# A routed expert layer: 28 tiles of 256 rows and 15 blocks of 128 rows in place of 39 tiles

## The chip, the core and the metric

The kernel runs on one core of one Trainium2 chip. The time is that of the device, in microseconds, for one launch. The kernel before took 417.74 us (median of 3 runs, 417.27 to 418.27).

## What is computed

`x` has 16 sequences of 256 tokens with 128 features, 4096 tokens in all. Everything is float32. One block of a transformer is computed: a modulated layer norm, a causal linear attention with 16 heads, a gated residual, and then the same around a layer of eight routed experts:

```python
h = rmsnorm(x @ W_in.T, in_norm_w)                 # 4096 x 128
logits = h @ Wr.T                                  # 4096 x 8
_, idx = top_k(logits + expert_bias, 2)            # two experts for each token
gates = softmax of the two chosen logits, else 0
for e in range(8):
    gate = silu(h @ Wg[e].T)                       # 128 -> 512
    up = h @ Wu[e].T                               # 128 -> 512
    oe = rmsnorm(gate * up @ Wd[e].T, enorm_w[e])  # 512 -> 128
    out = out + gates[:, e:e + 1] * oe
x = x + gb * (rmsnorm(out, out_norm_w) @ W_out.T)
```

The kernel computes an expert only for the tokens that chose it: 8192 rows (4096 tokens, two experts each). How many rows go to which expert is known only while the kernel runs.

## The kernel before

Three stages follow each other. **Attention and routing** goes through the 16 sequences in a software pipeline. It writes each normed row of a token, as a high and a low float16 half, into the DRAM buffer `dispatched` (`hbuf`), once for each of its two experts; every expert has a region of its own there. GpSimd does this with 64 indirect transfers of 128 rows (L547). **The expert stage** reads the rows back in tiles, computes gate, up and down, and writes the results to `expert_rows` (`ybuf`) in the order of the tokens. **The last stage** reads them in four transfers (L465), mixes the two results of a token, norms them and projects them.

**Tiles and tables.** A tile is `R = 256` rows of one expert. In the worst case the 8192 rows need `TILES = (8192 + 8*255) // 256 = 39` tiles, and always 39 are computed: unused ones read filler rows, whose results go to rows of `ybuf` that nobody reads. After the last sequence VectorE takes the counts of the experts (`total`, L1255), works out where each region ends (`tail`, L1257) and makes the table of tiles (L1260 to L1279: `tile_row`, the first row of each tile, and `tile_expert`). SyncE (L413) and ScalarE (L777) fill up the end of each region with 256 filler rows, 129 KB, in four transfers each. SyncE waits for all scatters, all filler and the table (L417 to L420), loads the table's rows into registers (L444 in the chain of waits) and starts on the tiles.

**The expert stage.** Its engines run the same order, written by hand, in turns of four tiles: a first turn, a loop `Fori(1, TURNS - 1)` and a last turn of three tiles. For a tile `t`:
- SyncE brings the 256 rows into SBUF turned by two DMA transposes, one for the high and one for the low half (L430), into slot `t % 4`, once tile `t - 4` no longer needs it. It also loads where the results go (`to_place`, L437).
- TensorE does `gate_up` (L1702) in halves of 256 of the 512 hidden columns: gate half 0, up half 0, gate half 1, up half 1. Each product of 128 hidden columns is three matmuls of 256 columns (high weights by high rows L1712, high by low L1713, low by high L1714): 24 of them in a tile. Then `down` (L1717) of tile `t - 1`: 24 matmuls of 128 columns (L1727 to L1729). Which weights are read depends on a register with the expert's number, so the addresses are worked out on the queue of TensorE as the kernel runs: the trace has register operations (ALU_OP, FUSED_REGOPS) under these lines.
- ScalarE does silu of a half (`gate`, L788), the high float16 half of the product (`high_part`, L794) and the sums of squares of the results of tile `t - 2` (`square`, L800).
- VectorE does the product of gate and up (`gated`, L1312), its low float16 half (`low_part`, L1319) and the scaling of the results (`weigh`, L1326).
- GpSimd scatters the results: two indirect transfers of 128 rows for each tile (L570).

G, U and Y are two PSUM banks each. TensorE may write a half of G or U when ScalarE and VectorE have read what stood in it two halves before.

## Time and profile before

| | us |
|---|---|
| median of 3 runs (lowest to highest) | 417.74 (417.27 to 418.27) |
| the profiled execution | 417.46 |
| its span, first to last instruction | 415.5 |
| from the start to the first matmul of the expert stage | 213.34 |
| from there to the start of its last matmul | 160.56 |
| after that | 41.6 |

The span is shown by the profile from its first to its last instruction; the execution took 1.96 us more. Busy time of an engine is that of its instructions. A matmul's duration is its way through the array, and several are under way at once: what a matmul costs in a dense row is the distance of the starts.

### The profile page before, as it was taken

The numbers are of one execution on the slowest core, as the hardware profiler recorded it, in microseconds if no ns is written. First come the engines' busy times: TensorE is split into PE (matmuls) and PEld (weight loads), VectorE is DVE, ScalarE is ACT, GpSimd is POOL, SyncE is SP. The second block draws the span as 40 slices with busy tenths as digits, with TensorE's granted clock in tenths as the row PEclk, the third lists the DMA queues.
The fourth block names the chain that finished last, engine by engine and source line by source line (L and its number), as shares of the span: only waits on it lengthen the run. The fifth ranks groups of instructions, "written<-read, shape, count | busy, mean of one in ns | idle before, by whom it ended". The sixth has DMA issues, their size and how long they took to land.

```text
span 415.5 us, 12907 instructions
## 1 busy us (share of the span) xinstructions
PE 353.6 (85%) x3750; PEld 308.6 (74%) x3751; DVE 321.0 (77%) x1029; ACT 292.0 (70%) x814; POOL 245.1 (59%) x221
## 2 busy tenths in 40 slices
PE   3799999999999999984049999999999999990464
PEld 2588887888888888873039989889899999980343
DVE  4078898899999999885828878787787778780686
ACT  4344769888888888744617778778778787873595
POOL 1957566788888888865541554554545455463341
PEclk9999999999999999995559999999999999997698
DMA  7997000000000000011412323233232232213833
GB/s 237 399 361 293 4 6 21 27 29 27 25 25 25 25 25 25 28 52 36 144 38 48 66 66 69 65 69 70 57 70 64 64 71 56 65 34 101 350 98 95
DMA packets 46563, 35.68 MB, mean 86 GB/s; under 512 B 36291, under 2 KB 42070, under 8 KB 45750
## 3 DMA queue, kind: packets, MB, share of 16 engines
q1 hardware_dynamic: 41718, 21.21, 18.4%
q0 software_dynamic: 4544, 9.39, 7.0%
q10 hardware_dynamic: 272, 4.72, 3.0%
q8 instruction: 15, 0.25, 0.3%
q14 instruction: 14, 0.11, 0.1%
HBM read 18.69 MB, written 13.47 MB: 77 GB/s over the span
## 4 chain that ended last, share of the span: by engine, by line
PE 52%; DVE 20%; issue 9%; DMA 8%; ACT 7%; POOL 2%; DVEq 1%; SPq 0%; ACTq 0%; POOLq 0%
PE bank L1712 9%; PE bank L1713 8%; PE bank L1714 8%; PE bank L1465 5%; DVE prod L953 4%; PE bank L1727 4%; PE bank L1729 4%; PE bank L1728 4%; DMA gates_bc<-gate_rows 4%; ACT junk L846 2%; PE bank L1543 2%; DVE st L877 1%; DVE rows L1014 1%; DVE wmaxs L1049 1%; DMA dispatched<-rows,pos 1%
## 5 line engine op out<-in xcount | busy, mean ns | idle before, releaser
L570 POOL DMA_INDIRECT expert_rows<-late,to_place x78 | 81.8, 1049 | 82.9 <-DVE late L1326 70.3
L1712 PE MATMUL bank<-late,w_hi 128*128 128x256 f16 x312 | 86.3, 277 | 14.8 <-DMA late<-dispatched 13.4
L1714 PE MATMUL bank<-late,w_lo 128*128 128x256 f16 x312 | 86.2, 276 | 0.0
L1713 PE MATMUL bank<-late,w_hi 128*128 128x256 f16 x312 | 86.2, 276 | 0.0
L1312 DVE SCALAR_TENSOR_TENSOR kv<-bank,uscale,kv 128x512 f32<-128x512 f32 x78 | 58.5, 750 | 32.1 <-ACT kv L788 18.6
L547 POOL DMA_INDIRECT dispatched<-rows,pos x64 | 67.3, 1051 | 26.7 <-issue 18.4
L529 POOL TENSOR_TENSOR kv<-kv,v 128x1024 f32<-128x1024 f32 x32 | 67.6, 2134 | 16.2 <-ACT kv L691 16.2
L1465 PE MATMUL bank<-cst,kv 128*128 128x128 f32 x576 | 74.6, 281 | 1.1 <-POOL kv L529 0.9
L1465 PEld LDWEIGHTS bank<-cst,kv 128*128 128x128 f32 x576 | 69.4, 195 | 1.8 <-POOL kv L529 1.0
L788 ACT ACTIVATE kv<-bank,descale 128x512 f32<-128x512 f32 x78 | 53.6, 687 | 23.3 <-PE bank L1714 19.3
L794 ACT ACTIVATE kv<-kv 128x512 f16<-128x512 f32 x78 | 48.8, 625 | 16.9 <-DVE kv L1312 11.4
L1319 DVE TENSOR_TENSOR kv<-kv 128x512 f16<-128x512 f32 x78 | 54.1, 693 | 5.6 <-ACT kv L794 3.6
L1727 PE MATMUL bank<-late,kv 128*128 x312 | 54.3, 219 | 0.5 <-DVE kv L1319 0.5
L1728 PE MATMUL bank<-late,kv 128*128 x312 | 54.3, 219 | 0.0
L1729 PE MATMUL bank<-late,kv 128*128 x312 | 54.3, 219 | 0.0
L953 DVE TENSOR_TENSOR prod<-bank,qT 128x384 f32<-128x384 f32 x96 | 49.6, 544 | 0.0
L1712 PEld LDWEIGHTS bank<-late,w_hi 128*128 x312 | 30.9, 99 | 20.1 <-issue 16.4
L1714 PEld LDWEIGHTS bank<-late,w_lo 128*128 x312 | 31.0, 99 | 3.9
L1713 PEld LDWEIGHTS bank<-late,w_hi 128*128 x312 | 31.0, 99 | 3.5
L612 ACT ACTIVATE xn<-x_all,nmr,rs 128x128 f32<-128x128 f32 (+1 forms) x64 | 27.8, 482 | 5.8 <-DVE nmr L894 5.5
L1727 PEld LDWEIGHTS bank<-late,kv 128*128 128x128 f16 x312 | 30.5, 98 | 1.1 <-issue 0.6
L1728 PEld LDWEIGHTS bank<-late,kv 128*128 128x128 f16 x312 | 30.5, 98 | 0.4
(231 smaller groups left out, 737.4 us busy)
## 6 DMA issues: line engine op xcount, KB each, us to landing
late<-wguT ACTq DMA_DIRECT2D x1, 4096.0 KB, 16.0
late<-expert_rows SPq DMA_DIRECT2D x1, 2064.0 KB, 11.0
gates_bc<-gate_rows SPq DMA_DIRECT2D x1, 2048.0 KB, 15.7
wd<-wdT SPq DMA_DIRECT2D x1, 2048.0 KB, 24.4
out<-kv SPq DMA_DIRECT2D x16, 128.0 KB, 1.8
late<-dispatched SPq DMA_TRANSPOSE x78
expert_rows<-late,to_place POOLq DMA_INDIRECT x78
late<-expert_rows SPq DMA_DIRECT2D x1, 1032.0 KB, 6.6
```

Source lines behind the costliest of these rows:

```text
L529: nc.gpsimd.tensor_tensor(kvt[:, 0:HD, :, :], k_in, v_in.to_broadcast([P, HD, H, HD]), ALU.mult).then_inc(kv_done[t], 1)
L547: pool.indirect_dma_start(hbuf, bass.IndirectOffsetOnAxis(ap=pos[:, p, t * K + k:t * K + k + 1], axis=0), rows[:, p, t, k, :], None).then_ ...
L570: pool.indirect_dma_start(ybuf, bass.IndirectOffsetOnAxis(ap=to_place[:, s, r:r + 1], axis=0), yt[:, s, r, :], None).then_inc(y_scat[s], 16)
L953: nc.vector.tensor_tensor(prod[:, t, cc * THIRD * P:(cc + 1) * THIRD * P].rearrange("p (e i) -> p e i", i=P), cum, qT[:, p, t * P:(t + 1) ...
L1312: nc.vector.scalar_tensor_tensor(gu[:, h, :], U[h], uscale[:], sg[:, h, :], ALU.mult, ALU.mult).then_inc(gu_done, 1)
L1465: last = mm(CUM[cc][:, j * P:(j + 1) * P], kv[:, p, t, e * D:(e + 1) * D], tri, start=True, stop=True)
L1712: mm(o, w_hi[:, w], hi, start=True, stop=False)
L1713: mm(o, w_hi[:, w], lo, start=False, stop=False)
L1714: last = mm(o, w_lo[:, w], hi, start=False, stop=True)
L1727: mm(o, gu_hi[:, s % 2, h, g], wd_hi[:, w], start=(f == 0 and r == 0), stop=False)
L1728: mm(o, gu_lo[:, s % 2, h, g], wd_hi[:, w], start=False, stop=False)
L1729: last = mm(o, gu_hi[:, s % 2, h, g], wd_lo[:, w], start=False, stop=(f == FC - 1 and r == RB - 1))
```

## The change

The expert stage computes 28 tiles of 256 rows (7 turns of four, the last turn being a turn like the others) and then 15 blocks of 128 rows. `TILES = (64 - 8) // 2 = 28`; `BLOCKS = (8192 + 8*127) // 128 - 56 = 15`. The regions' ends are filled with 128 rows. A tile now holds 256 rows only where the expert has more than 128 left for it. The 15 blocks have a table of their own, made by VectorE in 19 instructions behind the low halves of the down weights (L1284) and ahead of its first tile. The blocks are written out, not in a loop. On every engine their order is that of the tiles, one block in place of one half of a tile: TensorE does gate (12 matmuls of 128 columns), up (12) and then down of the block two before (12). The rows of a tile or block come by one DMA transpose for both halves. The weights' addresses are worked out in bytes. The diff below goes by engine: the constants; SyncE's filler (ScalarE's four transfers change alike), its tiles and its blocks; GpSimd, ScalarE, VectorE and TensorE.

```diff
-TILES = (TOK * K + E * (R - 1)) // R
-TURNS = -(-TILES // TURN)
-SPARE = TILES - TOK * K // R
+TILES = (TOK * K // P - E) // RB
+TURNS = TILES // TURN
+BLOCKS = (TOK * K + E * (P - 1)) // P - RB * TILES
+SPARE = (TOK * K + E * (P - 1)) // P - TOK * K // P
...
-    c[:, C_J:C_J + TOK // R] = np.arange(TOK // R) * R
+    c[:, C_J:C_J + TOK // R] = np.arange(TOK // R) * R + P
+    c[:, C_J0:C_J0 + TOK // R] = np.arange(TOK // R) * R
...
-                sp.dma_start(hbuf[bass.ds(row, R), :].rearrange("(p j) w -> p (j w)", p=16),
-                             filler[e * R:(e + 1) * R, :].rearrange("(p j) w -> p (j w)", p=16)).then_inc(filled, 16)
+                sp.dma_start(hbuf[bass.ds(row, P), :].rearrange("(p j) w -> p (j w)", p=16),
+                             filler[e * P:(e + 1) * P, :].rearrange("(p j) w -> p (j w)", p=16)).then_inc(filled, 16)
...
-                for half in range(2):
-                    sp.dma_start(hT3[:, s, half], hbuf16[bass.ds(row, R), half * D:(half + 1) * D],
-                                 transpose=True).then_inc(slot_ld[s], 16)
+                sp.dma_start(hT3[:, s], hbuf16[bass.ds(row, R), 0:2 * D], transpose=True).then_inc(slot_ld[s], 16)
...
+            def load_block(j, reg):
+                s = j % TURN
+                row = sp.snap(reg, min_val=0, max_val=HROWS - P)
+                sp.wait_ge(u3_ps, 2 * (TILES - TURN + j) + 2 if j < TURN else 2 * TILES + j - TURN + 1)
+                sp.dma_start(hT3[:, s, :, 0:P], hbuf16[bass.ds(row, P), 0:2 * D],
+                             transpose=True).then_inc(slot_ld[s], 16)
...
+            for j in range(BLOCKS):
+                s = j % TURN
+                pool.wait_ge(y_done[s], TURNS + j // TURN + 1)
+                pool.indirect_dma_start(
+                    ybuf, bass.IndirectOffsetOnAxis(ap=to_place[:, s, 0:1], axis=0),
+                    yt[:, s, 0, :], None).then_inc(y_scat[s], 16)
...
+            def block_gate(j):
+                act.wait_ge(g_ps, 2 * TILES + j + 1)
+                act.wait_ge(gu_done, 2 * TILES + j - 1)
+                nc.scalar.activation(sg[:, j % 2, :], G[j % 2], ACT.Silu, scale=descale[:]).then_inc(sg_done, 1)
+            def block_high(j):
+                act.wait_ge(gu_done, 2 * TILES + j + 1)
+                act.wait_ge(y_ps, TILES - 1 + j // 2 if j < TURN else TILES + j - TURN + 1)
+                nc.scalar.activation(gu_hi[:, j // 2 % 2, j % 2, :], gu[:, j % 2, :], ACT.Copy).then_inc(guhi_done, 1)
+            def block_square(j):
+                act.wait_ge(y_ps, TILES + j + 1)
+                act.wait_ge(ysq_done, RB * TILES + j)
+                nc.scalar.activation(junk3[:], Y[j % 2][:, 0:D], ACT.Square, scale=ydesc[:],
+                                     accum_out=yt[:, j % TURN, 0, D:YW]).then_inc(ysq_done, 1)
...
+            for j in range(2, BLOCKS):
+                block_high(j - 1)
+                if j == 2:
+                    for r in range(RB):
+                        square(TILES - 1, TURN - 1, TURNS - 1, r)
+                else:
+                    block_square(j - 3)
+                block_gate(j)
+            block_high(BLOCKS - 1)
+            for j in range(BLOCKS - 3, BLOCKS):
+                block_square(j)
...
+            for j in range(2, BLOCKS):
+                if j % TURN == 2:
+                    dve.load(block_ex[j // TURN % 2], block_expert[0:1, j - 2:j - 2 + TURN])
+                block_low(j - 1)
+                block_gated(j)
+                if j == 2:
+                    weigh(TILES - 1, TURN - 1, TURNS - 1, dve.snap(last_ex[1], min_val=0, max_val=E - 1))
+                else:
+                    block_weigh(j - 3, expert_of_block(j - 3))
...
+            def columns_of(w, e, per_expert, at):
+                return w.bitcast(U8)[:, bass.ds(e * (2 * per_expert) + 2 * at, 2 * P)].bitcast(F16)
...
-                    w = bass.ds(e * F + (part * E * F + (h * (FC // 2) + c) * P), P)
-                    mm(o, w_hi[:, w], hi, start=True, stop=False)
-                    mm(o, w_hi[:, w], lo, start=False, stop=False)
-                    last = mm(o, w_lo[:, w], hi, start=False, stop=True)
+                    wh, wl = (columns_of(w[:], e, F, part * E * F + (h * (FC // 2) + c) * P) for w in (w_hi, w_lo))
+                    mm(o, wh, hi, start=True, stop=False)
+                    mm(o, wh, lo, start=False, stop=False)
+                    last = mm(o, wl, hi, start=False, stop=True)
...
+            def block_gate_up(j, e, part):
+                s = j % TURN
+                if part == 0:
+                    pe.wait_ge(slot_ld[s], 16 * (TURNS + j // TURN + 1))
+                hi, lo = hT3[:, s, 0, 0:P], hT3[:, s, 1, 0:P]
+                pe.wait_ge((sg_done, gu_done)[part], 2 * TILES + j - 1)
+                for c in range(FC):
+                    o = (G, U)[part][j % 2][:, c * P:(c + 1) * P]
+                    wh, wl = (columns_of(w[:], e, F, part * E * F + c * P) for w in (w_hi, w_lo))
+                    mm(o, wh, hi, start=True, stop=False)
+                    mm(o, wh, lo, start=False, stop=False)
+                    last = mm(o, wl, hi, start=False, stop=True)
+                last.then_inc((g_ps, u3_ps)[part], 1)
+            def block_down(j, e):
+                pe.wait_ge(y_done[(j + 2) % TURN], TURNS + (j + 2) // TURN)
+                pe.wait_ge(gulo_done, 2 * TILES + j + 1)
+                o = Y[j % 2][:, 0:D]
+                for f in range(FC):
+                    g = slice(f * P, (f + 1) * P)
+                    hi, lo = gu_hi[:, j // 2 % 2, j % 2, g], gu_lo[:, j // 2 % 2, j % 2, g]
+                    wh, wl = (columns_of(w, e, FC * D, f * D) for w in (wd_hi, wd_lo))
+                    mm(o, hi, wh, start=(f == 0), stop=False)
+                    mm(o, lo, wh, start=False, stop=False)
+                    last = mm(o, hi, wl, start=False, stop=(f == FC - 1))
+                last.then_inc(y_ps, 1)
...
+            for j in range(BLOCKS):
+                if j % TURN == 0:
+                    pe.load(block_ex[j // TURN % 2], block_expert[0:1, j:j + TURN])
+                block_gate_up(j, expert_of_block(j), 0)
+                block_gate_up(j, expert_of_block(j), 1)
+                if j == 1:
+                    down(TILES - 1, TURN - 1, TURNS - 1, pe.snap(last_ex, min_val=0, max_val=E - 1))
+                elif j > 1:
+                    block_down(j - 2, expert_of_block(j - 2))
+            for j in range(BLOCKS - 2, BLOCKS):
+                block_down(j, expert_of_block(j))
```

## Rows read from the trace of the kernel before

**Rows 1.** The page: busy time by engine, with its share of the span and instructions.

```profile
PE 353.6 (85%) x3750; PEld 308.6 (74%) x3751; DVE 321.0 (77%) x1029; ACT 292.0 (70%) x814; POOL 245.1 (59%) x221
```

**Rows 2.** Stretches: busy us (and instructions) of each engine, granted clock, DMA.

```profile
193.00:213.00 20.00, 2.61 (x16) 1.66 (x13) 13.75 (x47) 8.07 (x14) 10.38 (x9) 0.50 0.29 90
230.60:327.80 97.20, 96.07 (x1152) 88.43 (x1152) 77.33 (x122) 77.66 (x193) 51.26 (x49) 1.00 0.31 66
327.80:374.20 46.40, 45.61 (x552) 41.92 (x552) 36.54 (x58) 36.64 (x94) 24.76 (x24) 1.00 0.25 56
...
392.60:413.00 20.40, 13.05 (x82) 9.83 (x82) 17.93 (x72) 17.16 (x79) 7.04 (x12) 1.00 0.32 92
```

**Rows 3.** Timeline of TensorE: start, us, engine, line, operation, what ended idle time.

```profile
214.16 0.42 PE L1713 MATMUL bank<-late,w_hi 128*128 128x256 f16 x1
...
285.80 0.27 PE L1714 MATMUL bank<-late,w_lo 128*128 128x256 f16 x1
285.91 0.22 PE L1727 MATMUL bank<-late,kv 128*128 x1
285.97 0.22 PE L1728 MATMUL bank<-late,kv 128*128 x1
...
327.86 0.28 PE L1712 MATMUL bank<-late,w_hi 128*128 128x256 f16 x1 [0.17 <-issue]
...
373.90 0.22 PE L1729 MATMUL bank<-late,kv 128*128 x1
```

**Rows 4.** Timelines of VectorE and ScalarE in one tile of the loop.

```profile
286.27 0.75 DVE L1312 SCALAR_TENSOR_TENSOR kv<-bank,uscale,kv 128x512 f32<-128x512 f32 x1
287.06 0.63 ACT L794 ACTIVATE kv<-kv 128x512 f16<-128x512 f32 x1 [0.40 <-DVE kv L1312]
287.61 0.37 ACT L800 ACTIVATE junk<-bank,ydesc 128x128 f32<-128x128 f32 x1
288.18 0.69 ACT L788 ACTIVATE kv<-bank,descale 128x512 f32<-128x512 f32 x1
288.97 0.75 DVE L1312 SCALAR_TENSOR_TENSOR kv<-bank,uscale,kv 128x512 f32<-128x512 f32 x1 [0.56 <-ACT kv L788]
```

**Rows 5.** TensorE's queue, 279.2 to 281.25: operation, count, duration ns, first and last start.

```profile
L1712 PEldq FUSED_REGOPS  x8: 46/46/46, 279.2 to 281.0; - x8
L1714 PEldq ALU_OP  x8: 32/32/36, 279.4 to 281.1; - x8
```

**Rows 6.** The same queue, table of experts, whole run.

```profile
L1698 PEldq TENSOR_LOAD <-tile_expert x10: 329/338/518, 205.4 to 359.2; - x10
```

**Rows 7.** The queue and the array at down's high weights (L1727), 281.2 to 282.5.

```profile
L1727 PEldq FUSED_REGOPS  x4: 46/46/46, 281.3 to 282.2; - x4
...
L1727 PE MATMUL bank<-late,kv x4: 219/219/219, 281.9 to 282.5; 128*128 x4
```

**Rows 8.** The chain of waits ahead of the expert stage: start, us, what.

```profile
204.20 4.89 DMA dispatched<-rows,pos
...
209.59 1.21 SPq L430
...
213.34 0.39 PE bank L1712
```

**Rows 9.** Issues that write `dispatched`, 199 to 209.4, and the page's median to landing.

```profile
L547 POOL DMA_INDIRECT dispatched<-rows,pos x5: 952/955/959, 198.3 to 204.2; - x5
L777 ACTq DMA_DIRECT2D dispatched<-filler x4: 530/619/657, 201.3 to 203.7; - x4
...
dispatched<-rows,pos POOLq DMA_INDIRECT x64, 2.3
```

**Rows 10.** Timeline of VectorE: the first tile's first product.

```profile
216.12 0.75 DVE L1312 SCALAR_TENSOR_TENSOR kv<-bank,uscale,kv 128x512 f32<-128x512 f32 x1 [6.00 <-PE bank L1714]
```

**Rows 11.** Timelines behind the last matmul: GpSimd, SyncE.

```profile
378.53 0.96 POOL L570 DMA_INDIRECT expert_rows<-late,to_place  x1 [0.30 <-issue]
...
381.16 1.77 SPq L465 DMA_DIRECT2D late<-expert_rows  x4
```

195 lines of the change are left out of this document (137 added, 58 removed).

## The prediction

> **What bounds the kernel now.** I read the busy times first. TensorE is busy 85% of the span, the most [rows 1], but that is an average over stages. By stretches, TensorE is busy 96.07 of 97.20 us inside the expert stage's loop at full clock [rows 2], with VectorE and ScalarE near 80%: this stage is bound by TensorE. Its timeline gives the price. A matmul of 256 columns starts 0.11 us after the one before, one of 128 columns 0.056 us after [rows 3]. A tile is 24 of each: 2.62 + 1.34 = 3.96 us. Over a turn of four come 0.2 to 0.3 us in which the queue loads the next experts (0.17 idle in the row at 327.86). The expert stage starts at 213.34, turn 7 (tile 28) at 327.86, and the last matmul ends at 373.90 + 0.22 = 374.12 [rows 3]. So the last 11 tiles, with one down carried over, cost 46.26 us.
>
> **Part 1: 11 tiles become 15 blocks.** By matmuls alone a block is 36 x 0.056 = 2.0 us, so 15 blocks with the carried down take 31.6 us and 14.7 us would be saved. I do not forecast that, because two things stand above 2.0 us.
>
> *The ring of ScalarE and VectorE.* In a block ScalarE does high(j-1), square(j-3), gate(j) and then at once high(j), which needs gated(j) of VectorE, which needs gate(j). No second half lies between, as in a tile. Start to start in the trace: gated to high 0.79, high to square 0.55, square to gate 0.57, gate to gated 0.79 [rows 4]. The ring is 2.70 us a block, and TensorE cannot go faster for long, as it has only two banks ahead.
>
> *TensorE's own queue.* Each product of three matmuls needs two register operations for its two weight addresses. In one tile's gate and up, 16 of them start within 1.9 us [rows 5], when nothing else held the queue: 0.24 us a product, 0.12 each, hardly depending on the matmuls between. In a tile this hides behind three matmuls of 256 columns, 0.33 us. In a block the three matmuls take 0.167 us, and the queue needs about 0.23. A block has 12 products, 24 operations. With 0.115 each (the rows hold waits too, so I go below 0.12): 2.76 us. Two places (start of gate, start of down) wait on two semaphores, so one wait stands as an instruction of its own; no row prices it, between nothing and one more 0.12; I take 0.10, near the register operations, 0.20 a block. Every fourth block the queue loads four experts, 0.34 us [rows 6], with the work on their numbers some 0.6 (estimated from the 0.2 to 0.3 us that a turn loses although the queue is ahead), so 0.15 a block. Sum 3.1; I take 3.05 us a block. Bytes in place of elements can turn the 46 ns operation into the 32 ns one [rows 5], 8 x 0.014 = 0.1 us a block, and two addresses a product remain. From below the ring bounds the block (2.70). From above, every operation is of the long kind and each of the three uses of a block's expert works out its own product: 24 x 0.13 + 0.2 + 0.15 = 3.5.
>
> So 15 x 3.05 = 45.75. Add the carried down (8 operations, 1.0). Subtract the lead that the queue has at that point: in the loop the first operation of down starts at 281.3 and its matmul at 281.9, the last at 282.2 for a matmul behind 282.5 [rows 7], 0.6 growing to some 0.8; I take 0.8. At the end down(14) waits for high and low of block 14, 0.35, and the last product drains, 0.25. Sum 46.55 against 46.26: **+0.3 us**. Seven row blocks fewer are computed, and the queue takes it back.
>
> VectorE and GpSimd keep up: one scatter of 0.96 + 0.30 us a block [rows 11] stands against 3.05.
>
> **Part 2: the first 28 tiles.** Their matmuls, waits and turns are the same; nothing on the path. SyncE's transposes are hidden there.
>
> **Part 3: half the filler.** The last scatter is issued at 204.20 and lands 4.89 us later [rows 8], where 2.3 is the median of 64 [rows 9]. What is new beside it are eight filler transfers of 129 KB, issued 201.3 to 203.7 [rows 9] (four by ScalarE, four alike by SyncE). With half the bytes the last scatter should land at its median, 206.5, the filler by 206.5 to 207.2. SyncE's wait ends up to 2.6 us earlier; I take **-2.2** (bounds -2.6 and 0).
>
> What is late next? The table of tiles is done at about 205, no. VectorE gets 19 small instructions (some 0.26 us each with their waits, 5 us) behind the low weights, in front of its first product. It has 6.00 us of idle there [rows 10]. With the start 2.6 us earlier it is late by 1 to 2 us, but TensorE needs that product only when up of tile 1 begins, 3 us after it is done now, so nothing. If that cover were gone: up to 1.5 us, once.
>
> **Part 4: one transpose.** The first tile waits for two issues, of 1.21 us and as much again, and landing [rows 8]. If one issue of 1.2 carries both halves, the first tile comes 1.2 us earlier; if its length goes with the rows of each half, nothing, and a little later if a half can no longer start alone (+0.3). I take **-0.4**.
>
> Here a rule of the Trainium skill can be weighed: "DMA: Bandwidth & Descriptors", Rules for kernel authors, says to coalesce many small transfers, since small ones mostly pay overhead. By it the whole second issue would go, and the sum would be 0.8 us lower. The rows only show that a transfer of 1.2 us issue is not followed at once by its data; they cannot decide it.
>
> **Part 5: the tail.** The last two scatters belong to the last tile, and GpSimd was a tile behind: the last begins at 378.53, 4.41 us after the last matmul [rows 3, 11]. After, the last block has one scatter. Its square takes 0.57 [rows 4], its weigh, half as wide as a tile's, some 0.35 (an estimate), and it finds GpSimd with at most one scatter in front: it begins 1.5 us after the last matmul. **-2.9** (bounds -3.2 and -1.5). From there on (378.53 to the load at 381.16 [rows 11] and the last stage) nothing changes.
>
> **Sum.** 0.3 - 2.2 - 0.4 - 2.9 = -5.2 us. The rows come from an execution of 417.46 us (span 415.5), 0.28 below the median: **412.3 us**.
>
> **Rivals.**
> - *The ring alone bounds a block* (queue cheaper than I read it, for instance one address operation a product). 15 x 2.70 + 0.8 = 41.3, -5.0; with the rest -5.5: 407.0 us. For: the ring's steps are rows. Against: nothing in [rows 5] shows a product with one operation. 0.22.
> - *The clock falls in the blocks*, the case on the other side. TensorE would have some 65% of its time filled, with short gaps at each product. At the lower level, 1.2 GHz, a matmul of 256 columns costs 0.21 us (the row at 214.16) [rows 3], one of 128 columns 0.107, and a block 36 x 0.107 = 3.85 us. 15 x 3.85 + 0.8 = 58.6, +12.3, minus 5.5: 424.3 us. It decides from about a third of the blocks at that clock, where 5.5 us are eaten. Against: from 392.6 to 413.0 TensorE is busy 13.05 of 20.40 us, 64%, at clock 1.00, while the clock of 0.50 goes with 2.61 of 20 us [rows 2]. 0.08. The Trainium skill speaks for it: "TensorE: Matmul & The Clock Gate", A second HAM failure mode: psum-queue depth-cycling, tells of a kernel whose brief idling between groups of matmuls made the clock swing between the two levels. The stretch at 392.6 does not bear that out here.
> - *The queue is dearer* (3.4 us a block: all operations of the long kind, products worked out anew, or the straight code of 15 blocks fetched too slowly). 51.8, +5.6, and the gain is gone: 417.5 us. For: the waits and the table are estimates, a tenth of the 3.05. Against: in the last turn, straight code too, TensorE stayed dense (the stretch from 327.80) [rows 2]. 0.14; beyond 3.5 us a block it would be slower.
> - *The front gives nothing* (the scatter's 4.89 us are not the filler's): 412.3 + 2.6 = 414.9 us. 0.06.
>
> The forecast keeps 0.50, with a range of its own from 410.3 to 415.0 (2.9 to 3.25 us a block).
>
> **Chances.** A measurement of this kernel can tell about 0.2%, 0.8 us. Faster: 0.50 + 0.22 + 0.06 and a fifth of the dear queue, 0.81. Same: 0.07, from the dear queue. Slower: 0.12, the clock and the dearest queue. The range that should hold 8 in 10 reaches from the ring with a full front, 406.3, to the dear queue, 417.5.
>
> **What would show it.** In the changed kernel the block stretch has a clock of 1.00 and matmuls in threes: 0.056, 0.056, then a gap, 0.23 us from first to first, with idle time put down to "issue" on TensorE or its weight loads; blocks start 3.05 us apart. If they stand 2.70 apart with the idle time behind ScalarE and VectorE, the ring was right. Blocks of 2.0 us would show both wrong. The first transpose should be issued near 207.4, the first matmul stand near 210.7, and the last scatter begin 1.5 us behind the last matmul. The forecast is wrong if the clock in the blocks shows 0.50, or if more than two register operations stand with a product.

## The result: 422.89 us in place of 417.5

The changed kernel took 422.89 us (median of 4 runs, 421.76 to 423.84), the kernel before, on the same chip, 417.5. The ratio is 1.010, with an interval of 1.006 to 1.015 (the two medians alone would give 1.013, inside it): slower by 1%, where I had forecast 412.3 us. The profiled execution took 423.49 us with a span of 421.7, 6.1 more than the span of before. The two traces, cut at the same points:

| stretch, us | before | after | difference |
|---|---|---|---|
| start to VectorE's copy of the counts (attention stage, unchanged) | 200.03 | 201.11 | +1.08 |
| to the first expert matmul | 13.31 | 11.00 | -2.31 |
| to the first matmul of tile 28, or of block 0 | 114.52 | 116.36 | +1.84 |
| to the end of the last expert matmul | 46.26 | 52.69 | +6.43 |
| to the first load of `expert_rows` | 7.04 | 4.31 | -2.73 |
| last stage | 34.36 | 36.19 | +1.83 |

### The profile page after: what moved, and what is told of

Read it like the earlier page. It is cut to its first block, busy times and chain, and to the rows that moved or that the text cites. A ratio compares the mean times of both kernels' runs of the same rounds, so it can differ in the third digit from the quotient of the medians.

```text
span 421.7 us, 12899 instructions
## 1 busy us (share of the span) xinstructions
PE 358.5 (85%) x3762; PEld 307.4 (73%) x3763; DVE 317.7 (75%) x1036; ACT 281.3 (67%) x786; POOL 237.3 (56%) x214
## 4 chain that ended last, share of the span: by engine, by line
PE 51%; DVE 24%; issue 9%; DMA 6%; ACT 6%; POOL 2%; DVEq 1%; ACTq 0%; POOLq 0%; SPq 0%
PE bank L1856 6%; PE bank L1858 6%; PE bank L1857 6%; PE bank L1605 4%; DVE prod L1023 4%; PE bank L1910 4%; DMA gates_bc<-gate_rows 4%; PE bank L1871 3%; PE bank L1872 3%; PE bank L1873 3%; PE bank L1912 2%; PE bank L1923 2%; PE bank L1911 2%; PE bank L1683 2%; DVE st L947 1%
## 5 line engine op out<-in xcount | busy, mean ns | idle before, releaser
L1856 PE MATMUL bank<-late,w_hi 128*128 128x256 f16 x224 | 62.5, 279 | 13.8 <-DMA late<-dispatched 11.0
L1858 PE MATMUL bank<-late,w_lo 128*128 128x256 f16 x224 | 62.4, 279 | 0.0
L1857 PE MATMUL bank<-late,w_hi 128*128 128x256 f16 x224 | 62.4, 279 | 0.0
L1412 DVE SCALAR_TENSOR_TENSOR kv<-bank,uscale,kv 128x512 f32<-128x512 f32 x56 | 41.8, 750 | 16.7 <-ACT kv L829 11.4
L829 ACT ACTIVATE kv<-bank,descale 128x512 f32<-128x512 f32 x56 | 38.3, 686 | 16.6 <-PE bank L1858 13.9
L835 ACT ACTIVATE kv<-kv 128x512 f16<-128x512 f32 x56 | 35.0, 626 | 14.8 <-DVE kv L1412 12.3
L1419 DVE TENSOR_TENSOR kv<-kv 128x512 f16<-128x512 f32 x56 | 38.8, 694 | 4.5 <-ACT kv L835 3.3
L1871 PE MATMUL bank<-late,kv 128*128 x224 | 39.0, 219 | 0.1
L1873 PE MATMUL bank<-late,kv 128*128 x224 | 39.0, 219 | 0.0
L1872 PE MATMUL bank<-late,kv 128*128 x224 | 39.0, 219 | 0.0
L1856 PEld LDWEIGHTS bank<-late,w_hi 128*128 x224 | 22.4, 100 | 17.9 <-issue 15.2
L1910 PE MATMUL bank<-late,w_hi 128*128 128x128 f16 x120 | 26.1, 219 | 2.9 <-issue 1.6
L1911 PE MATMUL bank<-late,w_hi 128*128 128x128 f16 x120 | 26.0, 218 | 0.0
L1912 PE MATMUL bank<-late,w_lo 128*128 128x128 f16 x120 | 25.9, 217 | 0.0
```

Of the source, the lines that this page charges most:

```text
L1856: mm(o, wh, hi, start=True, stop=False)
L1857: mm(o, wh, lo, start=False, stop=False)
L1858: last = mm(o, wl, hi, start=False, stop=True)
L1871: mm(o, gu_hi[:, s % 2, h, g], wh, start=(f == 0 and r == 0), stop=False)
L1872: mm(o, gu_lo[:, s % 2, h, g], wh, start=False, stop=False)
L1873: last = mm(o, gu_hi[:, s % 2, h, g], wl, start=False, stop=(f == FC - 1 and r == RB - 1))
```

## The profile after, against that of before

The page has hardly changed: TensorE at 85%, VectorE now at 75%.

```profile
PE 358.5 (85%) x3762; PEld 307.4 (73%) x3763; DVE 317.7 (75%) x1036; ACT 281.3 (67%) x786; POOL 237.3 (56%) x214
```

The stretches say where to look (busy us and instructions of PE, PEld, DVE, ACT, POOL; granted clock; DMA share and GB/s). They answer to [rows 2].

```profile
230.60:328.00 97.40, 96.38 (x1161) 88.83 (x1159) 77.61 (x123) 77.77 (x193) 51.13 (x48) 1.00 0.32 64
333.60:350.50 16.90, 15.49 (x187) 12.29 (x185) 8.85 (x15) 8.67 (x22) 7.19 (x7) 1.00 0.33 46
350.50:367.40 16.90, 15.24 (x178) 11.90 (x177) 8.16 (x16) 8.32 (x20) 4.79 (x5) 1.00 0.20 44
385.30:402.30 17.00, 8.14 (x35) 7.15 (x36) 8.87 (x34) 9.14 (x42) 4.96 (x8) 0.50 0.70 274
...
405.70:409.10 3.40, 3.19 (x15) 2.80 (x15) 2.73 (x12) 3.02 (x15) 1.58 (x3) 0.51 0.28 80
```

The tiles are as dense as before. In the blocks the clock is 1.00, so the clock does not bound a block. VectorE and ScalarE are idle half of the time; that alone would not rule their ring out, since two engines that wait for each other are both idle in turn. But no idle time of TensorE in the blocks is put down to them, only to "issue" (1.6 us from 333.6 to 374). TensorE looks 91% busy only because a matmul's 0.22 us on the array overlaps the next: 187 matmuls, at the 0.056 us of [rows 3], would need 10.5 of the 16.9 us. The last two lines are the last stage: its low clock lasts 17.0 us and comes back for 3.4, where before it was 13.6 us (379.0 to 392.6). Both kernels also end in a low stretch.

The timeline of TensorE (start, us, what, idle time and its cause) from block 0 to the last matmul; it answers to [rows 3].

```profile
328.47 0.22 PE L1910 MATMUL bank<-late,w_hi 128*128 128x128 f16 x1
...
341.02 0.23 PE L1910 MATMUL bank<-late,w_hi 128*128 128x128 f16 x1 [0.49 <-issue]
341.09 0.22 PE L1911 MATMUL bank<-late,w_hi 128*128 128x128 f16 x1
341.14 0.22 PE L1912 MATMUL bank<-late,w_lo 128*128 128x128 f16 x1
341.25 0.22 PE L1910 MATMUL bank<-late,w_hi 128*128 128x128 f16 x1
...
347.79 0.23 PE L1910 MATMUL bank<-late,w_hi 128*128 128x128 f16 x1
...
380.94 0.22 PE L1925 MATMUL bank<-late,kv 128*128 x1
```

Products start 0.23 us apart (341.02, 341.25), as predicted. Two blocks take 6.77 us (341.02 to 347.79), 3.39 each; those with a read of the table take 3.7 to 3.8. The average from block 4 on is 3.45 us.

What stood in TensorE's queue besides, all 15 blocks together (operation, count, ns least/median/most, first and last start); it answers to [rows 5, 6].

```profile
L1932 PEldq MOVE  x45: 29/29/38, 328.1 to 379.8; - x45
L1905 PEldq EVENT_SEMAPHORE  x15: 51/51/51, 328.2 to 375.3; - x15
L1917 PEldq EVENT_SEMAPHORE  x15: 51/51/51, 335.9 to 379.9; - x15
L1936 PEldq TENSOR_LOAD <-block_expert x4: 329/335/340, 327.7 to 368.0; - x4
L1910 PEldq FUSED_REGOPS  x30: 37/37/37, 328.3 to 376.4; - x30
L1912 PEldq ALU_OP  x120: 32/32/36, 328.4 to 377.2; - x120
```

A block has three MOVE (L1932 is the snap of the expert's number), two EVENT_SEMAPHORE (the waits of L1905 and L1917), 3 FUSED_REGOPS and 21 ALU_OP. The durations are not what they cost. From the start of one record of the queue to the start of the next, averaged over eight blocks (27.7 us): a weight load 0.037 us, an ALU_OP 0.061, FUSED_REGOPS 0.087, MOVE 0.088, EVENT_SEMAPHORE 0.114, TENSOR_LOAD 0.39. So 36 x 0.037 + 21 x 0.061 + 3 x 0.087 + 3 x 0.088 + 2 x 0.114 + 0.10 = 3.47 us a block. That this sum meets the time proves nothing: distances from start to start fill the time whatever the queue waits for. What speaks for the queue as the bound is that they hardly vary: each ALU_OP takes 60 or 61 ns, each MOVE 87 or 88, and 14 of the 16 EVENT_SEMAPHORE 106. Only the weight loads vary, from 13 to 208 ns; three in a block are followed by 57 ns or more, 0.18 us a block above the others (an estimate from these distances), and why stays open. Runs 5 to 9 test the rest.

Now the front. The timelines of VectorE, GpSimd and TensorE; they answer to [rows 10].

```profile
210.25 0.28 DVE L1360 TENSOR_TENSOR prod<-total,cst 1x128 f32<-1x128 f32 x1
210.57 0.27 DVE L1362 TENSOR_REDUCE nhalf<-prod 1x8 f32<-1x128 f32 x1
210.88 4.05 DVE L1363 TENSOR_SCALAR rest<-tstart 1x8 f32<-1x8 f32 x1
214.96 0.15 DVE L1364 SCALAR_TENSOR_TENSOR paired<-tend,rest 1x8 f32<-1x8 f32 x1
...
218.30 0.16 DVE L1384 SCALAR_TENSOR_TENSOR block_row<-cst,brow 1x16 int32<-1x16 f32 x1
219.28 1.41 DVE L1412 SCALAR_TENSOR_TENSOR kv<-bank,uscale,kv 128x512 f32<-128x512 f32 x2 [0.81 <-issue]
...
210.35 4.55 POOL L598 TENSOR_TENSOR gates_bc<-gates_bc,woutn 128x2048 f32<-128x2048 f32 x1 [4.07 <-DVE late L1353]
...
220.16 0.27 PE L1856 MATMUL bank<-late,w_hi 128*128 128x256 f16 x1 [1.74 <-DVE kv L1412]
```

One instruction on 8 numbers took 4.05 us. It ended at 214.93, when GpSimd's product of 128 x 2048 ended (214.90). That product stood there before too (210.27, 4.49 us), but VectorE was idle then. Now the table of the blocks is done at 218.46, the first product of gate and up starts at 219.28 in place of 216.12, and TensorE waits 1.74 us. This wait is what stands in the third row of the table of stretches (+1.84), where I had forecast nothing.

TensorE's first expert matmul (the first line, of its timeline) stands on its transfer, as before. But the chain of waits no longer goes through it: at this place it follows VectorE (the other lines). It answers to [rows 8].

```profile
212.11 0.39 PE L1856 MATMUL bank<-late,w_hi 128*128 128x256 f16 x1 [11.04 <-DMA late<-dispatched]
...
210.88 4.06 DVE rest L1363
219.28 0.76 DVE kv L1412
```

The transposes before tile 4, one in place of two, each as long to issue as one of two before:

```profile
L442 SPq DMA_TRANSPOSE late<-dispatched x4: 1186/1200/1312, 209.2 to 213.9; - x4
```

And the tail on the timelines of GpSimd and SyncE, which answers to [rows 11]: the last scatter starts 1.62 us after the end of the last matmul (381.16), where it was 4.41.

```profile
381.51 0.96 POOL L617 DMA_INDIRECT expert_rows<-late,to_place  x1 [0.30 <-issue]
382.78 0.96 POOL L617 DMA_INDIRECT expert_rows<-late,to_place  x1 [0.30 <-issue]
...
385.47 0.81 SPq L502 DMA_DIRECT2D late<-expert_rows  x2
```

## The experiments

They change the changed kernel, unless they say otherwise. Their ratios are to the kernel before on the same chip. "Front" is the time from the copy of the counts to the first matmul of tile 2, counting tiles from 0 (22.43 us before, 22.35 after), "block stage" that from the first matmul of tile 28 or block 0 to the end of the last (46.26 and 52.69).

| kernel | us | ratio, interval | front | blocks, mean from block 4 on |
|---|---|---|---|---|
| 1 another form | 422.93 | 1.010, 1.006 to 1.014 | 22.29 | 3.45 |
| 2 GpSimd later | 419.97 | 1.001, 0.999 to 1.004 | 20.30 | 3.45 |
| 3 filler of 256 | 424.08 | 1.011, 1.006 to 1.015 | 22.36 | 3.45 |
| 4 two transposes | 423.09 | 1.009, 1.006 to 1.012 | 22.35 | 3.59 |
| 5 light queue | 418.86 | 0.998, 0.994 to 1.002 | 24.00 | 3.04 |
| 6 snaps alone | 420.84 | 1.005, 1.003 to 1.008 | 22.36 | 3.18 |
| 7 waits alone | 420.80 | 1.006, 1.003 to 1.008 | 22.35 | 3.22 |
| 8 elements | 427.69 | 1.020, 1.015 to 1.025 | 24.03 | 3.64 |
| 9 fixed expert | 413.68 | 0.986, 0.982 to 0.991 | 22.35 | 2.96 |
| 10 fixed, scatter's wait moved | 415.67 | 0.992, 0.988 to 0.995 | 24.01 | 3.06 |
| 11 changed kernel again | 422.97 | 1.009, 1.006 to 1.013 | 24.02 | 3.45 |
| 12 kernel before again | 430.66 | 1.002, 0.998 to 1.006 | 22.36 | |
| 13 both repairs | 425.44 | 0.989, 0.985 to 0.992 | 20.29 | 3.16 |
| 14 and scatter's wait moved | 426.17 | 0.989, 0.986 to 0.992 | 20.29 | 3.11 |
| 15 and gate ahead of square | 426.14 | 0.990, 0.986 to 0.994 | 20.30 | 3.09 |

Kernels 12 to 15 ran on a chip on which the kernel before took 430.83 us; for the other experiments it took 418.2 to 419.1.

### 1. Is it the form of VectorE's instruction?

```diff
-            then(nc.vector.tensor_scalar(rest[:], tstart[:], float(TILES), None, ALU.min))
+            then(nc.vector.scalar_tensor_tensor(rest[:], tstart[:], float(TILES), tstart[:], ALU.min, ALU.min))
```

> The changed kernel with one instruction of the table of blocks written in another form: the minimum with 28 over 8 numbers (tensor_scalar, 4.05 us in the trace of after, beside 0.15 for its neighbours) becomes a scalar_tensor_tensor with the same result. Theory A (the tensor_scalar waits for GpSimd's product over 128x2048, 210.35 to 214.90, and only this form does): the instruction takes about 0.15 us, the table is done near 214.4, the 1.74 us that TensorE waits at 218.14 for VectorE go: 2 us faster than the changed kernel, near 421.0. Theory B (any instruction at that place is held, for instance by the memory that GpSimd writes): the 4 us move to the new instruction or its neighbour, no change of the time.

The timelines of VectorE and GpSimd:

```profile
210.56 4.04 DVE L1363 SCALAR_TENSOR_TENSOR rest<-tstart 1x8 f32<-1x8 f32 x1
...
210.03 4.55 POOL L598 TENSOR_TENSOR gates_bc<-gates_bc,woutn 128x2048 f32<-128x2048 f32 x1 [4.06 <-DVE late L1353]
```

Held all the same. It is not one form of instruction that is held: the other form was held just as long, while a TENSOR_REDUCE (L1362, 210.57) passed beside GpSimd's product. The Trainium skill tells of this, "SBUF — State Buffer", section Who interferes with whom: VectorE and GpSimd share one pair of SBUF ports, which one of them has at a time, and a VectorE instruction needs it in its two-port mode or with two SBUF inputs. The 4.04 and 4.05 us agree with it.

### 2. GpSimd's product behind the table

```diff
             pool.wait_ge(wdlo_done, DN)
+            pool.wait_ge(block_table, 1)
```

> The changed kernel in which GpSimd's product over 128x2048 (4.55 us, the gates of the last stage) waits for the table of blocks as well. In the changed kernel and in e1_port one instruction of the table stands for 4.04 us and ends when that product ends, in both of its forms. Theory A (VectorE and GpSimd hold each other off there): the table takes 4 us instead of 8, is done near 214.3, TensorE's idle time at 218.1 (1.74 us) goes, and with it the fall of the clock that followed it in e3 and e4: 2 us faster than the changed kernel or a little more, near 420.5, and its runs lie closer together. Rival: the product then holds off the first low parts, and TensorE waits for them instead: no gain.

The timelines of GpSimd and VectorE:

```profile
214.39 4.52 POOL L599 TENSOR_TENSOR gates_bc<-gates_bc,woutn 128x2048 f32<-128x2048 f32 x1 [8.48 <-DVE block_row L1385]
...
210.51 0.16 DVE L1364 TENSOR_SCALAR rest<-tstart 1x8 f32<-1x8 f32 x1
...
215.03 0.75 DVE L1413 SCALAR_TENSOR_TENSOR kv<-bank,uscale,kv 128x512 f32<-128x512 f32 x1 [0.81 <-PE bank L1859]
...
217.55 2.50 DVE L1420 TENSOR_TENSOR kv<-kv 128x512 f16<-128x512 f32 x2
```

The instruction takes 0.16 us, all 19 take 4.4, the first product starts at 215.03, the front is 2.05 us shorter. The hold moved to where it is cheap: two low halves took 2.50 us, where two take 1.47 or less elsewhere. The ratio falls by 0.009, 3.7 us. That is more than the 2.05 of the front in the two profiles, but the two intervals, each of some 0.003 to 0.004 to either side, leave room for 2.05 as well; run 11 shows one thing that can make up the rest.

### 3 and 4. What did the front's two edits give?

Run 3 fills up with 256 rows again (ScalarE's transfers change alike), run 4 brings the halves by a transpose each (in the blocks too).

```diff
-                sp.dma_start(hbuf[bass.ds(row, P), :].rearrange("(p j) w -> p (j w)", p=16),
+                sp.dma_start(hbuf[bass.ds(row, R), :].rearrange("(p j) w -> p (j w)", p=16),
```

```diff
-                sp.dma_start(hT3[:, s], hbuf16[bass.ds(row, R), 0:2 * D], transpose=True).then_inc(slot_ld[s], 16)
+                for half in range(2):
+                    sp.dma_start(hT3[:, s, half], hbuf16[bass.ds(row, R), half * D:(half + 1) * D],
+                                 transpose=True).then_inc(slot_ld[s], 16)
```

> The changed kernel with 256 filler rows for each region's end, as before: twice the bytes in the eight filler transfers, the same tables, tiles and blocks. Theory A (the filler's bytes hold up the last scatter and SyncE's wait): from the counts' copy on VectorE to the first transpose 9.5 us as before, in place of 8.05 to 8.3, so 1.3 us later; TensorE's wait for VectorE behind it shrinks, so the whole is at most 1 us slower. Rival (the last scatter's landing has another cause): the first transpose stays at 8.1 us.

> The changed kernel with two transposes for each tile and block, as before. In the traces one issue of both halves takes 1.2 us, one of a single half 1.15 us. Theory A (the first tile waits for two issues one after the other): the first matmul comes 1.2 us later after the first issue, TensorE's wait for VectorE behind it shrinks by as much, so the kernel is within 1 us of the changed kernel. Rival: SyncE becomes late in the blocks (2.3 us of issues and 0.4 for the places in 3.4 us): slower by more.

Counted from the copy of the counts: with full filler the first transpose is issued at 9.46 us in place of 8.05 and the first matmul stands at 12.38 in place of 11.00, so the filler is worth 1.4 us. With two transposes the first matmul is 3.75 us behind the first issue in place of 2.95, so the one transpose is worth 0.8. But tile 2 starts at 22.36 and 22.35, as in the changed kernel (22.35): VectorE sets that time. Both gains are there, and neither reaches the end. With the hold gone, in run 2, the front is 20.30, 2.13 below the kernel before.

The rival of run 4, that SyncE becomes late in the blocks, came true in part. TensorE's waits in its blocks:

```profile
PE bank L1913 <- DMA late<-dispatched: 2.7, 5, 0.8
```

Its block stage took 54.13 us in place of 52.69. The ratio (1.009) does not show this 1.4 us; the profiled execution, 426.63 us, was one of the slowest of its ten. So what the one transpose spares SyncE in the blocks may be worth more than what it gives at the front, and one profile does not settle it.

### 5 to 7. What is in the queue?

Run 6 makes the first change (the snaps, down to the first cut), run 7 the second (the waits), run 5 both (the diff is cut to its core; down's uses of the number change like gate's):

```diff
+                if j % TURN == 0:
+                    block_e[j:j + TURN] = [pe.snap(r, min_val=0, max_val=E - 1) for r in block_ex[j // TURN % 2]]
-                block_gate_up(j, expert_of_block(j), 0)
+                block_gate_up(j, block_e[j], 0)
...
-                if part == 0:
+                if part == 0 and j < 3:
                     pe.wait_ge(slot_ld[s], 16 * (TURNS + j // TURN + 1))
...
+                    if part and j >= 2 and c == FC - 1:
+                        pe.wait_ge(y_done[j % TURN], TURNS + j // TURN)
...
-                pe.wait_ge(y_done[(j + 2) % TURN], TURNS + (j + 2) // TURN)
+                if j >= BLOCKS - 2:
+                    pe.wait_ge(y_done[(j + 2) % TURN], TURNS + (j + 2) // TURN)
...
+                    if f == FC - 1 and j + 3 < BLOCKS:
+                        pe.wait_ge(slot_ld[(j + 3) % TURN], 16 * (TURNS + (j + 3) // TURN + 1))
```

> The changed kernel with a lighter queue in the blocks: the experts' numbers are taken over once for four blocks behind the table read, not three times a block, and the two second waits of a block (slot loaded, results read) are put one product earlier, where they ride on a register operation. 24 address operations remain. By the gaps in the trace of after, three moves at 0.088 and two semaphore instructions at 0.106 go, 0.47 us a block, and about 0.1 comes back with the work on four numbers at once. Theory A (the queue bounds a block): blocks about 3.05 us apart, 15 x 0.37 = 5.5 us faster than the changed kernel, near 417. Theory C (another wait bounds them): no change.

> Only the copies of the expert's number are changed: one snap of four registers for four blocks in place of three snaps in each block; the waits stay. In the changed kernel the trace has three MOVE at the uses of the number, 0.0875 us from each to the next operation, 0.26 us a block. Theory A (each operation of the queue costs its own time and they add up): blocks 0.26 - 0.09 = 0.17 us shorter, 3.26 on the average, 2.6 us in all, ratio 1.004. Rival B (each snap also makes the compiler work out the product with the expert's stride anew, so products go with the snaps): FUSED_REGOPS or ALU_OP fewer than 24 a block too, 0.3 us or more, ratio 1.000 or less, nearly all that the light queue gave.

> Only the separate waits are moved: those for the transposed rows and for the free slot stand ahead of a later product, where the instruction behind has its one wait free. In the changed kernel two EVENT_SEMAPHORE stand in a block, 0.106 us from each to the next operation. Theory A (they add up): blocks 0.21 us shorter, 3.2 on the average, 3.2 us in all, ratio 1.002. Rival B (the waits cost nothing on their own, the queue only stands there until the semaphore it asks for has come): blocks as in the changed kernel within 0.05 us, ratio 1.010.

The block stage: 52.69 us in the changed kernel, 47.6 with both, 49.3 with the snaps alone and 49.9 with the waits alone (first matmul of block 0 to the end of the last). A block is 0.27 us shorter by the snaps, 0.23 by the waits and 0.40 by both. The queue of run 6, gate's high weights:

```profile
L1910 PEldq ALU_OP  x105: 32/32/32, 331.1 to 376.2; - x105
L1910 PEldq FUSED_REGOPS  x15: 37/37/37, 330.9 to 374.5; - x15
```

All MOVE are gone, not two of three, and half of the FUSED_REGOPS here became ALU_OP; the count of address operations is still 24 a block. So theory A counted too few copies, and rival B, by which whole products would go, is wrong. For the waits theory A held in the blocks (0.21 expected); its ratio of 1.002 lies below the interval. Both together give less than their sum: at 2.9 us other things begin to stand in the way (one weight load of run 5 had 0.40 us to the next record, where 0.21 was the most in the changed kernel), and every read of the table still costs half a us (3.4 us blocks among those of 2.9).

### 8. Bytes undone

```diff
-                    wh, wl = (columns_of(w[:], e, F, part * E * F + c * P) for w in (w_hi, w_lo))
+                    w = bass.ds(e * F + (part * E * F + c * P), P)
+                    wh, wl = w_hi[:, w], w_lo[:, w]
...
```

Down and the tiles change alike.

> The changed kernel with the weights addressed in elements again, as before, in tiles and blocks. Theory A (each register operation costs the queue a fixed part and its own length, 0.113 for the 32 ns form and 0.124 for the 46 ns form): if the first address of each product turns into the 46 ns form, 12 x 0.012 = 0.14 us a block, 2 us slower than the changed kernel; if all 24 do, 4 us slower. Tiles stay at 3.96 us either way. Rival: bytes change nothing that is measured, within 0.5 us.

Blocks of 3.64 in place of 3.45 us, 3 us in all. The queue at gate's and up's high and low weights:

```profile
L1913 PEldq FUSED_REGOPS  x120: 46/46/65, 331.0 to 382.5; - x120
L1915 PEldq ALU_OP  x120: 32/32/36, 331.2 to 382.6; - x120
```

The operation of every high weight of gate and up (8 a block) is now the long form, and so are all 8 of down: 16 a block, where bytes leave 3 of the shorter fused form. From its start to the next record's start it takes 0.096 us, an ALU_OP 0.060. But the weight load behind a long form starts the next record sooner (0.029 us on the average in place of 0.037), so the prices do not simply add up. Bytes help, and more than the 0.1 us a block that I had put on them from the durations.

### 9 and 10. No address work at all

In run 9 TensorE reads expert 0's weights in all blocks, so its queue has no address to work out: the choice of the expert is left out of the blocks. Run 10 leaves it out too, and the wait for an earlier scatter goes from VectorE's low half to ScalarE's square. (Down's weights change alike.)

```diff
-                block_gate_up(j, expert_of_block(j), 0)
+                block_gate_up(j, 0, 0)
...
-                    wh, wl = (columns_of(w[:], e, F, part * E * F + c * P) for w in (w_hi, w_lo))
+                    wh, wl = (w[:, part * E * F + c * P:part * E * F + (c + 1) * P] for w in (w_hi, w_lo))
```

> The changed kernel in which TensorE's blocks read the weights of expert 0, at addresses fixed when the kernel is built (it leaves out the choice of the expert in the blocks; matmuls, waits and rows are the same). No register operation and no table read is left in the blocks. Theory A (TensorE's queue bounds a block at 3.4 us; next comes the ring of ScalarE and VectorE): blocks start 2.7 us apart, 15 x 0.7 = 10.5 us faster than the changed kernel, near 412. Theory B (the ring is hidden too, the matmuls are next): 2.0 us apart, 21 us faster, near 402. Theory C (the ring or another wait bounds the blocks already, the queue only looks busy): still 3.3 us apart and no gain.

> The kernel e2_static (TensorE's blocks read the weights of expert 0 at fixed addresses, so it leaves out their choice) with one wait moved: that the scatter of the block four before has landed is waited for by ScalarE ahead of its square, not by VectorE ahead of its low part. In e2_static blocks were 2.9 us apart on average and uneven (2.0 to 4.2), with VectorE waiting up to 2.16 us for the landing. Theory A (queue, then scatter, then the ring): blocks an even 2.7 us apart, 15 x 0.25 = 3.5 us faster than e2_static, near 410. Rival (the unevenness is the clock's fall at 357 or SyncE): 2.9 on average again.

Run 9's waits of VectorE and TensorE in the blocks (us in total, times, longest), and TensorE, SyncE and ScalarE on run 10's timelines:

```profile
DVE kv L1464 <- DMA expert_rows<-late,to_place: 7.1, 5, 2.2
PE bank L1910 <- DMA late<-dispatched: 5.0, 6, 2.0
```

```profile
349.47 0.29 PE L1910 MATMUL bank<-late,w_hi 128*128 128x128 f16 x1 [4.55 <-DMA late<-dispatched]
...
339.94 1.18 SPq L473 DMA_TRANSPOSE late<-dispatched  x1
343.70 0.34 SPq L480 DMA_DIRECT2D to_place<-dispatched  x1
344.23 1.18 SPq L473 DMA_TRANSPOSE late<-dispatched  x1
...
341.21 0.63 ACT L874 ACTIVATE kv<-kv 128x512 f16<-128x512 f32 x1 [0.92 <-DVE kv L1459]
343.69 0.63 ACT L874 ACTIVATE kv<-kv 128x512 f16<-128x512 f32 x1 [0.92 <-DVE kv L1459]
```

The queue is confirmed as the bound: without its address work, copies and table reads the kernel is 2.4% faster than with them. But neither run shows even blocks of 2.7 us. In run 9 blocks come 2.0 to 4.2 us apart: a low half waits up to 2.2 us until the scatter that used its slot has landed, TensorE waits up to 2.0 us for transposed rows, and its clock is 0.50 from 357.3 to 360.7. Moving the low half's wait did not give the 3.5 us that I expected: run 10 was no faster (ratio 0.992 after 0.986, intervals that overlap), its blocks 3.06 after 2.96 us. What remains is SyncE: its load of the places (L480) waits for the same landing, and the transpose behind it in its queue comes late, 344.23 after 339.94; TensorE waits 4.55 us, and its clock is 0.50 from 347.8 to 354.6. No run moves SyncE's wait, so this part is read from the trace and not tested. The ring itself runs at 2.48 us where it is undisturbed (341.21 to 343.69, high to high), not at my 2.70. So the order below the queue's 3.4 is: landings of the scatters and SyncE's order, and only then the ring. In the changed kernel VectorE already waits for such landings (3.3 us in three waits, the longest 1.6), without holding up TensorE.

### 11 and 12. Both kernels again

Neither is edited.

> The changed kernel once more, unchanged. Theory A: first to last matmul of the expert stage 169.0 within 1 us and blocks of 3.3 us with 3.7 to 3.8 at each read of the table, as in its first profile; the copy of the counts and the last stage may differ from the first profile by 1 to 2 us (201.11 and 36.2 there). Ratio to before 1.010. Rival B: the blocks' 3.43 were peculiar to one execution: another mean by over 0.1 us.

> The kernel before once more, unchanged, as a yardstick. In the runs so far the copy of the counts came anywhere from 200.6 to 203.2 us, and the last stage took 34.3 to 36.3 us, with an early stretch at clock 0.50 of 13.6 to 17 us. Theory A (these differences belong to the execution, not to the change): this profile also shows a copy of the counts somewhere in 200 to 203 and a last stage in 34 to 36.5, while first to last matmul of the expert stage stays at 160.8 within 0.3. Rival B (the change causes them): copy at 200.0 and last stage at 34.3 within 0.2, as in the first profile of before.

The changed kernel again: blocks the same to 0.01 us, the copy of the counts at 201.84, a last stage of 34.98 us (36.2 in the first profile). But the front took 24.02 us, and with it first to last matmul took 170.7, where 169.0 within 1 us was expected. TensorE waited 2.07 us for VectorE at 220.90, and then the clock fell once more:

```profile
218.10:221.50 3.40, 1.33 (x13) 0.96 (x11) 2.42 (x8) 0.67 (x2) 0.00 (x0) 1.00 0.23 39
221.50:224.90 3.40, 3.40 (x21) 2.59 (x20) 2.54 (x4) 2.38 (x4) 0.00 (x0) 0.50 0.02 5
```

At 0.50 TensorE has 21 matmuls in 3.40 us. The front has three values in all these runs: 20.3 us in the four kernels in which GpSimd comes later, 22.3 to 22.4 with the hold, 24.0 with the hold and the fall (runs 5, 8, 10, 11). So the hold costs 2.05 or 3.7 us, by execution. The spread of the runs fits: run 2's twelve lie within 2.0 us, the eight of the changed kernel here within 3.3. The length of the wait does not decide it alone: in run 6 TensorE waited longer at this place, and the clock stayed at 1.00 until 381.4.

```profile
222.64 0.27 PE L1856 MATMUL bank<-late,w_hi 128*128 128x256 f16 x1 [3.14 <-DVE kv L1412]
```

The kernel before again, on the slower chip: its copy of the counts came at 208.95, its last stage took 35.05 us with the clock low from 391.2 to 411.7 (20.5 us), first to last matmul 164.7 in place of 160.8. Theory A's numbers for the copy of the counts and for first to last matmul are wrong for this chip. Its point stands in part: the last stage's first low stretch varies from 13.7 to 20.5 us among the changed kernels (13.7 in the changed kernel itself, here) and is 13.6 and 20.5 in the two profiles of the kernel before. So I count neither the +1.83 of the last stage nor the +1.08 of the attention stage as the change's. That is a choice: two profiles of before, on two chips, do not show that the change adds nothing there.

### 13 to 15. Repairs together

Run 13 is run 2 with run 5's edits. Run 14 adds the moved wait of run 10. Run 15 adds this:

```diff
                 block_high(j - 1)
+                block_gate(j)
                 if j == 2:
...
                     block_square(j - 3)
-                block_gate(j)
```

> Two repairs of the changed kernel together: GpSimd's product behind VectorE's table, and the light queue (one snap of the numbers for four blocks, the second waits moved). Theory A (two separate costs, added up): against the changed kernel -3.7 us of the one and -3.3 to -4 of the other, about 415.5 us where before has 419, ratio 0.991; first to last matmul of the expert stage near 163, blocks 2.9 us apart, the first turn as with GpSimd later (second tile near 9.5 to 10 us behind). Rival B (both pay in the same idle time, or the clock falls again at the start as in the light-queue run): 419 us, first turn 11 or more, a stretch of clock 0.50 near 221.

> As the two repairs together, and the low half of a block no longer waits for the scatter that has its slot of the results (the square waits for it, later in the block). Theory A (with the queue at 2.9 us a block a scatter has long landed when its slot comes round): within 0.5 us of the two repairs together, blocks 2.9 apart and even. Rival B (landing waits already touch blocks of 2.9, as they did those of 2.47 to 2.7 with a fixed expert): 0.5 to 2 us faster than the two repairs together.

> As the one before, with ScalarE doing the gate of a block ahead of the square of the block three before. Theory A (TensorE's queue bounds the block at 2.9, the ring of ScalarE and VectorE measured 2.47): no difference beyond 0.5 us. Rival B (the ring at 2.70, as I worked out from the tiles, touches blocks where the queue has run ahead): 1 us or more faster. Either way, if both repairs add up, the ratio to before is near 0.99.

Run 13 has a ratio of 0.989, 1.1% below the kernel before on its chip, which is shown. By the ratios it is 2.1% below the changed kernel, where 0.9% and 1.2% were found apart, so the two repairs seem to add up; but the changed kernel did not run on this chip, and on it the kernel before lost 3.9 us in its own expert stage. Theory A's ratio was right; its 163 us from first to last matmul was not (165.5, in the slowest of its six executions): some blocks waited, and the clock fell in the blocks. The waits of TensorE in the blocks of run 13, and the stretch at the low clock:

```profile
PE bank L1913 <- DVE late L1427: 1.0, 1, 1.0
PE bank L1929 <- DMA late<-dispatched: 0.9, 1, 0.9
...
348.70:352.10 3.40, 3.40 (x35) 3.38 (x33) 0.84 (x2) 1.46 (x4) 1.89 (x2) 0.50 0.30 81
```

Moving the scatter's wait and putting the gate first change nothing that can be told (0.989 and 0.990, intervals nearly the same), as theory A said for both: at 2.9 us a block the queue is still what bounds. Run 13 is the version to keep: it beats the kernel before, and by the ratios the changed one.

## Why the prediction was wrong

**The forecast's sum was -5.2 us, the traces' is about +3.2, or +4.9 when the clock falls, and the ratio says +4.3.** Two steps failed, two held.

- **The block stage (part 1): +0.3 forecast, +6.4 measured.** The bound was named rightly, TensorE's queue and not its matmuls, and a product's 0.23 us was right. The failed step is "I take 3.05 us a block", a term that was too small: it measured 3.45. Missing were the copies of the expert's number: three snaps, 0.26 us, which no row of before had made me look for. They stood only inside my upper bound of 3.5, as products worked out anew. The two waits cost 0.23 (0.20 taken). The 24 address operations with their weight loads came to 2.9 (2.76 taken; 16 starts within 1.9 us are 15 distances of 0.127 us, so the row said 0.127, not 0.12, before anything was taken off for waits), the table to 0.10 spread over four blocks (0.15 taken), but its blocks are 0.4 us longer. Runs 6 and 7 show the first two by taking them away. The rival "the queue is dearer" had 3.4 us a block, 51.8 for the stage, and met it within 1 us; I gave it 0.14.
- **VectorE's table (part 3): "so nothing" forecast, +2.05 to +3.7 measured.** This is the second failed step. I priced 19 instructions by the usual duration, 5 us, and set them against 6.00 us of idle [rows 10]. I did not look at what GpSimd did in that idle time. Its product of 4.5 us held one of the 19 for 4.05 us, and the cover was gone by 3. I had capped the case "cover gone" at 1.5 us. Run 2 takes the hold away, and there the 19 instructions took 4.4 us: the price was right, the cover was not.
- **Half the filler and one transpose: -2.6 forecast for the first matmul, -2.3 measured.** Right in sum, though not in parts: the filler gives 1.4 (2.2 taken), the transpose 0.8 (0.4 taken). A single issue of 1.20 us carries both halves where one half had taken 1.21 [rows 8]. The Trainium skill's rule on coalescing ("DMA: Bandwidth & Descriptors", Rules for kernel authors) points the same way, and the trace agrees: 0.8 us, between my 0.4 and the 1.2 of a whole issue. But I asked what is late next and answered "no": the gain ends in TensorE's wait for VectorE, and the front is 22.35 us after 22.43. The rival "the front gives nothing" came true by another mechanism than its own.
- **The tail: -2.9 forecast, -2.73 measured.** Right, by the predicted 1.5 us from the last matmul to the last scatter (1.62).
- **The clock in the blocks** stayed at 1.00, as I held against that rival. It fell at the front, in some executions, behind the wait for VectorE. It did fall in the shorter blocks of runs 9, 10 and 13 for 3.4 to 6.8 us, so this rival is not dead for kernels with a lighter queue.
- **The ring** is 2.48 us, not 2.70, and did not bind the changed kernel.

The other side's price was wrong as well as its chance: queue at 3.4 and front at nothing are two cases that I never added to each other, and their sum (417.5 + 2.6 = 420.1) lies above the top of my range, though still below the measured 422.89. (The forecast's own range was also worked out 0.3 us too narrow at each end: 2.9 and 3.25 us a block give 410.0 and 415.3.)

## What to carry to other kernels

Where a matmul's address depends on a register, count all that the queue issues for a unit of work, weight loads, copies, waits and address operations, each by the distance of starts and not by its duration, and then take one of them away to see whether the time follows. Halving the rows of a unit halves the matmuls' time but not that count. Idle time on VectorE is not free cover while GpSimd works on SBUF: look at the neighbour's timeline before putting instructions there. And after each gain at a front, follow the next wait to its end before it enters the sum.

## What was not expected of the hardware

- A register operation of 32 ns costs TensorE's queue 0.061 us, a fused one of 37 ns 0.087 and one of 46 ns 0.095, a copy of 29 ns 0.088, a separate wait of 51 ns 0.106 when it finds its semaphore set, a load of four numbers of 335 ns 0.39.
- A VectorE instruction on 8 numbers was held for 4.04 and 4.05 us by one of GpSimd's, in two forms; one already begun (L1360) and a reduction (L1362) were not.
- After TensorE's wait of 2.07 us at the front the clock fell to 0.50 from 221.5 to 224.9; after one of 1.74 us in another execution, and one of 3.14 us in run 6, it did not. What decides that stays open.
